# Batch-norm factors behind the second tT split, and squares fetched behind their own store

## The reference

```python
# x, ctx: (16, 256, 512); w_q, w_k, w_v, w_o: (512, 512)
q, k, v = x @ w_q.T, ctx @ w_k.T, ctx @ w_v.T
probs = softmax(q @ k.T / sqrt(512))
x = x + alpha * (probs @ v) @ w_o.T
# second layer: 1x1 convolutions over 256 channels, 128 inner channels, 512 positions
g_x, phi_x = conv(g_w, g_b, ctx).T, conv(phi_w, phi_b, ctx)
theta_x = conv(theta_w, theta_b, x).T
y = ((theta_x @ phi_x / 512) @ g_x).T
wy = conv(w_w, w_b, y)
wy = bn_gamma * (wy - bn_mean) * rsqrt(bn_var + 1e-5) + bn_beta
out = wy + x
```

## Time and profile before

| | us |
|---|---|
| median of 3 runs (394.41 to 394.79) | 394.48 |
| the profiled execution | 395.11 |
| its span in the trace | 393.3 |
| TensorE (PE) busy in the span | 385.5 (98%) |
| VectorE (DVE) busy | 291.3 (74%) |
| ScalarE (ACT) busy | 187.4 (48%) |
| pairs 2 to 6, one loop turn | about 44.6 |

### The profile page before, as it was taken

One profiled execution on the slowest core, in us unless ns is written; L12 is line 12 of the kernel. 1 busy time (PEld: TensorE's weight loads), 2 busy tenths in 40 slices (PEclk: granted clock), 3 DMA queues, 4 the chain that ended last, 5 costly groups with the idle time before them and its releaser, 6 DMA issues.

```text
span 393.3 us, 5832 instructions
## 1 busy us (share of the span) xinstructions
PE 385.5 (98%) x1978; PEld 329.3 (84%) x1978; DVE 291.3 (74%) x570; ACT 187.4 (48%) x387; POOL 1.4 (0%) x7
## 2 busy tenths in 40 slices
PE   8999999999999999999999999999999999999994
PEld 5887888889878898889888898889888898889874
DVE  5898557987489756995678856895678955996585
ACT  4476443662466237441566238451575237551341
POOL 1000000000000000000000000000000000000000
PEclk9999999999999999999999999999999999999999
DMA  7984740576553555546553565555554463024512
GB/s 237 378 332 162 263 133 27 173 255 208 168 214 108 210 183 178 172 165 207 166 208 112 187 202 169 168 181 194 175 188 136 170 204 105 27 80 165 161 50 107
DMA packets 56220, 68.13 MB, mean 173 GB/s; under 512 B 4625, under 2 KB 47121, under 8 KB 53137
## 3 DMA queue, kind: packets, MB, share of 16 engines
q1 hardware_dynamic: 56064, 67.72, 52.1%
q10 hardware_dynamic: 144, 0.26, 0.2%
HBM read 49.09 MB, written 18.87 MB: 173 GB/s over the span
## 4 chain that ended last, share of the span: by engine, by line
PE 88%; DVE 4%; SPq 3%; DMA 2%; ACT 2%; issue 1%; DVEq 0%; ACTq 0%
PE bank L328 23%; PE bank L329 23%; PE bank L330 23%; PE bank L390 6%; PE bank L378 4%; PE bank L379 4%; PE bank L380 4%; DMA cT_raw<-ctx_t 2%; SPq L193 2%; DVE xb L898 1%; DVE ov_lo L808 1%; ACT c_sides L549 1%; DVE gram_blocks L793 0%; DVE x_lo L741 0%; DVE xb L924 0%
## 5 line engine op out<-in xcount | busy, mean ns | idle before, releaser
L328 PE MATMUL bank<-ov_hi,c_sides 128*128 128x512 f32 x128 | 50.0, 390 | 0.0
L329 PE MATMUL bank<-ov_lo,c_sides 128*128 128x512 f32 x128 | 50.0, 390 | 0.0
L329 PE MATMUL bank<-c_sides,qk_hi 128*128 128x512 f32 x128 | 50.0, 390 | 0.0
L330 PE MATMUL bank<-c_sides,qk_lo 128*128 128x512 f32 x128 | 49.9, 390 | 0.0
L328 PE MATMUL bank<-c_sides,qk_hi 128*128 128x512 f32 x128 | 49.8, 389 | 0.0
L330 PE MATMUL bank<-ov_hi,c_sides 128*128 128x512 f32 x128 | 49.8, 389 | 0.0
L630 ACT ACTIVATE probs<-bank,neg_max 128x256 f32<-128x256 f32 x32 | 14.9, 471 | 56.9 <-DVE neg_max L844 56.9
L549 ACT ACTIVATE x_hi<-xb 128x512 fp32r<-128x512 f32 x32 | 20.0, 633 | 35.1 <-DVE xb L898 35.1
L378 PE MATMUL bank<-tT_hi,xT_hi 128*128 128x256 f32 x128 | 36.3, 283 | 0.1
L379 PE MATMUL bank<-tT_lo,xT_hi 128*128 128x256 f32 x128 | 36.2, 283 | 0.0
L380 PE MATMUL bank<-tT_hi,xT_lo 128*128 128x256 f32 x128 | 36.2, 283 | 0.0
(11 more groups left out here) (131 smaller groups left out, 880.3 us busy)
## 6 DMA issues: line engine op xcount, KB each, us to landing
cT_raw<-ctx_t SPq DMA_DIRECT2D x8, 1024.0 KB, 4.9
xT_raw<-x_t SPq DMA_DIRECT2D x8, 1024.0 KB, 4.8
c_raw<-ctx_n SPq DMA_DIRECT2D x8, 1024.0 KB, 5.0
xb<-x SPq DMA_DIRECT2D x16, 512.0 KB, 4.0
out<-xb SPq DMA_DIRECT2D x15, 512.0 KB, 2.7
gram_moved<-gram_blocks SPq DMA_DIRECT2D x16, 256.0 KB, 2.3
gram_blocks<-gram_moved SPq DMA_DIRECT2D x64, 64.0 KB, 2.1
moved<-blocks SPq DMA_DIRECT2D x16, 256.0 KB, 2.4
```

Source lines behind the costliest of these rows:

```text
L328: pe.matmul(dst, ahi, bhi, start=(k == 0), stop=False)
L329: pe.matmul(dst, ahi, blo, start=False, stop=False)
L330: mm = pe.matmul(dst, alo, bhi, start=False, stop=(k == k_tiles - 1))
```

## The change

Three things. In the setup the seven small operations on the batch-norm factors move on DVE from ahead of ov_lo to behind tT_part(1), and the two rows that they use move from the buffer of gram_blocks to that of probs. In pairs 1 to 7, SP waits for the store of batch 0's squares and issues its four fetches before it sends batch 1's squares; pair 0 keeps both sends first. In pairs 1 to 6 ACT runs c_sums ahead of t1_part instead of behind it.

```diff
@@ -94,7 +94,7 @@
-        setup_rows = gram_blocks[:].rearrange("p b j x a -> p (b j x a)")
+        setup_rows = probs[:].rearrange("p b t s -> p (b t s)")
         std_row, bn_row = setup_rows[:, 0:L], setup_rows[:, L:2 * L]
@@ -267,10 +267,13 @@
                 for b in range(2):
                     sp.wait_ge(blocks_made, two[b + 1])
                     send(moved[b], blocks[:, b], blocks_stored[b])
-                for b in range(2):
-                    sp.wait_ge(blocks_stored[b], turned[16])
-                    fetch(pT_raw[:, b], moved[b], pT_loaded[b])
-                if first:
+                    if not first:
+                        sp.wait_ge(blocks_stored[b], turned[16])
+                        fetch(pT_raw[:, b], moved[b], pT_loaded[b])
+                if first:
+                    for b in range(2):
+                        sp.wait_ge(blocks_stored[b], turned[16])
+                        fetch(pT_raw[:, b], moved[b], pT_loaded[b])
                     sp.wait_ge(phi_blocks_made, two[2])
                     send(phi_moved, phi_blocks[:], phi_stored)
                     fetch_phi()
@@ -680,10 +683,10 @@
                 vo_part(0, 1)
                 pT_part(0)
                 if not first:
+                    if not last:
+                        c_sums(loads[32])
                     t1_part(0)
                     t1_part(1)
-                    if not last:
-                        c_sums(loads[32])
                 pT_part(1)
@@ -792,6 +795,17 @@
             dve.wait_ge(std_made, 2)
             dve.reciprocal(bn_row, std_row).then_inc(bn_step, 1)
             dve.reciprocal(bn_col[:], std_col[:]).then_inc(bn_step, 1)
+            for m in range(KH):
+                dve.wait_ge(ov_hi, m + 1)
+                dve.scalar_tensor_tensor(out=ov[1][:, m, :], in0=bank[KH + m][:], scalar=row[:, ROW_ALPHA:ROW_ALPHA + 1],
+                                         in1=ov[0][:, m, :].bitcast(F32), op0=ALU.mult,
+                                         op1=ALU.subtract).then_inc(ov_lo, 1)
+            gram_squares(0, [1, 2], 1)
+            tT_part(0, 1)
+            for b in range(2):
+                xT_part(b, b + 1)
+            gram_squares(1, [3, 4], 2)
+            tT_part(1, 2)
             dve.wait_ge(bn_step, 3)
...
@@ -803,17 +817,7 @@
             dve.wait_ge(bn_step, 8)
-            for m in range(KH):
-                dve.wait_ge(ov_hi, m + 1)
-                dve.scalar_tensor_tensor(out=ov[1][:, m, :], in0=bank[KH + m][:], scalar=row[:, ROW_ALPHA:ROW_ALPHA + 1],
-                                         in1=ov[0][:, m, :].bitcast(F32), op0=ALU.mult,
-                                         op1=ALU.subtract).then_inc(ov_lo, 1)
-            gram_squares(0, [1, 2], 1)
-            tT_part(0, 1)
-            for b in range(2):
-                xT_part(b, b + 1)
-            gram_squares(1, [3, 4], 2)
-            for m in range(1, KH):
+            for m in range(2, KH):
                 tT_part(m, m + 1)
```

## The result

| | before | after |
|---|---|---|
| median of 22 runs of each, side by side | 394.60 us | 393.81 us |
| lowest and highest run | 394.19 to 396.12 | 393.16 to 395.90 |
| profiled execution, its span | 395.11, 393.3 | 394.11, 392.3 |

The ratio is 0.9979, with a 95% interval of 0.9972 to 0.9986: faster by 0.79 us, where 1.68 under the 394.48 known then was forecast. The sign holds, and so do the chains that the prediction read in pairs 1 and 7. The size doesn't: less than half came, and the first place where it is missing is the setup. The time itself lies in the stated range (392.2 to 394.0), close to the rivals 3 and 4 (393.7 and 393.6), but neither of the two is what happened, as will be seen: pair 1's stall is gone, and no split holds the scores back.

The account below looks back on a forecast made before the run. TensorE (PE) was taken to bound the kernel, with gains only where it stands still: in the setup and pair 1. -0.86 - 0.95 + 0.05 = -1.76 us took 394.48 to 392.7, stated as 392.8; range 392.2 to 394.0.

Parts of the forecast that it names:

- the chains that the prediction read in pairs 1 and 7: Store, fetch and split order up to vo_lo: ready at 110.2 in pair 1 (PE asks at 110.41), 378.8 in pair 7.
- rivals 3 and 4: 3: pair 1's stall stays, 393.7, chance 0.10. 4: setup splits hold the scores, only pair 1 gains, 393.6, chance 0.06.
- pair 1's stall: PE waits for vo_lo of the second batch before delta(1): 0.98 us, with the restart 1.10 together.
- Part 1, -0.86: Setup: without the batch-norm operations ahead, ov_lo is ready before PE asks; wait of 0.72 plus restart of 0.14 goes.
- Part 2, within -0.95: Pair 1: sums fill ACT's idle time, so the stall before delta(1) goes; -0.95 us, between 0 and -1.10.
- the stall named "issue": PE's 0.8 us wait called "issue" in pair 1, read as a wait for vo_lo of the second batch.
- Part 3, +0.05: Pair 7: batch 1's squares come later behind the chained store and fetches, delaying vo_lo to 378.8; +0.05 us.
- The chain of 7.54 us: SP after store 0 lands: four fetch issues 1.82, store 1 2.35, three issues 1.37, a fetch's landing 2.0.
- The second rival: Serial chain about 0.4 us slower: pair 1 keeps about 0.35 of its stall, pair 7 pays 0.35; 393.5, chance 0.14.
- The sixth: Slower: store 1 beside batch 0's fetches takes 4.4 us instead of 2.35, squares 2 us late; 398.5, chance 0.09.
- The sum.: Whole kernel: -0.86 - 0.95 + 0.05 = -1.76 us, from 394.48 to 392.7, stated as 392.8.
- The steady pairs: Pairs where PE is busy throughout: they stay at 44.6 us, edits under PE's cover being worth nothing.

Follow-up runs that it names:

- the two timed pairs: Batch-norm operations moved behind the second tT split: on the kernel before, 394.74 us against 394.95; on the kernel with c_sums already ahead of t1_part, 393.74 against 393.97.
- sums_only: Only c_sums moved ahead of t1_part, against the kernel before: 393.97 us against 394.95, ratio 0.9981.
- x_late_only: Kernel before with the load of the next x (batch 0) moved behind the eight fetches in pairs 1 to 7: 394.18 us against 394.92, ratio 0.9983.
- after_again: The changed kernel, unchanged, run and profiled once more against the kernel before: 394.19 us against 394.92, ratio 0.9976.
- before_again: The kernel before, unchanged, profiled once more: profiled execution of 395.13 us, span 393.3.
- the three parts timed alone: Each of the three edits alone on the kernel before (394.95 us): batch-norm move 394.74, c_sums first 393.97, fetches behind their own store 395.02.

## Why the prediction was off, step by step

**Part 1, -0.86.** This is the step that failed. The chain was read rightly: ov_lo did start as soon as it could, no wait took its place, and the moved operations cost nothing (they run on DVE at 38.39 to 39.67 after the change). But "PE could have gone on at 30.82" and ov_lo's end at 31.49 were taken as fixed points, and the wait is the difference of the two. Over the six profiles with the old setup PE asks at 30.75 to 31.84, and ov_lo starts at 28.51 to 29.22. The old wait had absorbed whatever lateness PE had by then. With it gone, that lateness shows. Kernels with the old setup start their scores at 43.06, 43.51, 42.80, 43.31, 43.44 and 43.06, on average 43.20; those with the new one at 42.97, 43.20, 43.01, 42.78, 42.93 and 42.56, on average 42.91. The term measures -0.3 from profiles and -0.2 to -0.4 from the two timed pairs. In parts: the wait is gone whole, as said, but it was worth 0.57 on average (0 to 1.28) and not 0.86; and PE starts both_rows(0) 0.28 later in the six kernels with part 1. That second half rests on six profiles against six, whose ranges overlap; whether it is chance or comes with part 1 stays open. The measured -0.3 lies between the prediction's bounds (0 if another wait takes its place, 0.86 if none does), but for neither of their reasons: no wait takes its place, and the wait itself is smaller.

**Part 2, within -0.95.** The chain was read rightly down to the last link, the stall named "issue" included, and sums_only and x_late_only show it from both sides. In the executions profiled it came whole: 71.17 before, 70.10 after. Mis-sized for the timed runs: the profiled execution had 1.09 us in this stall, the average of seven is 0.73. There the first fetches landed late: from the store's issue to pT_hi(0) 8.03 us, in the nine others with that load ahead 7.5 to 7.7.

**Part 3, +0.05.** The chain of 7.54 us behind the first fetch was measured as 7.47 in pair 1, and in pair 7 as 375.37 - 367.84 = 7.53 (after) and 7.50 (after_again). The mis-sized term lies ahead of it: store 0's landing, taken as 4.4 as in the one profile, was 4.3, 4.7 and 5.1 in the three profiles with part 3, and the tail paid 0.05, 0.15 and 0.53. The second rival had the effect (later squares, pair 7 pays), but from the wrong transfer. The sixth, a second store as slow as the first, did not come: it lands in 2.3 to 2.6.
The Trainium skill's page "DMA: Bandwidth & Descriptors", in the anatomy of a DMA, would have store 1 land in 2.6, an estimate from a fit for the software path. In pairs 1 and 7 here it took 2.34 to 2.67 from its issue to the next fetch, mostly a little under the page; neither number decides the result.

**The sum.** -0.3 - 0.73 + 0.24 (the mean of three tails) = -0.8, the measured -0.79. That it fits so closely is luck: each term is a mean of a few profiles, and the three parts timed alone add up to -1.1 by their medians. The prediction had a warning and made the wrong use of it. It noted that the profiled execution was 0.6 us above the median and carried every term over unchanged. The part behind pair 1's Gram is the same to 0.03 us in all profiles without part 3, so the extra time of a slower profiled execution lies ahead of it, where both waits are. It need not lie in the waits themselves: before_again took 395.13 too, with 0.28 and 0.66 in them, because PE was late already at both_rows(0).

**What held.** The steady pairs: 44.60 of 44.60 us busy before and after. The moved operations, the rows in another buffer, the later x load and the sooner load_c were all free, as said.

## What to carry to other kernels

A wait that one profile shows on the fastest engine is worth its length only if both its ends are steady from execution to execution: look for what each end depends on (here the landing of the first weights, and the pace of the first products), and price the wait as a range down to zero where one end is loose. When the profiled execution is slower than the median, ask first where its extra time lies before carrying the sizes of its waits over. And where two transfers are independent, as the two stores here, issue both before either is waited for: chained, they brought nothing in pairs 1 to 6 and passed on up to 0.53 us of a late landing in pair 7.

## What the runs showed of the hardware

A store of 256 KB issued 1.4 to 2.3 us behind a load of 512 KB took 2.4 to 5.1 us to land, most in pairs 1 and 7 (before and the three profiles with part 3). With that load moved behind it, at the same place of the code, it took 2.3 in pairs 1 to 6 and 2.9 in pair 7 (x_late_only). Moving the load alone is worth 0.7 us, about as much as the whole change.

TensorE's first weight products after eight idle ones take anything from 1.00 to 1.85 us for four, between one execution and the next, while the interval from pair 1's Gram products to the last rows repeats to 0.03 us in 274 where part 3 is absent. Without the idle products it is 1.85 for the first four in both profiles, and the kernel is 1.8 us slower.
